# Moving the closing VectorE pair of each scan tile behind the next tile's product, in a Mamba and MoE layer

## The reference

```python
DS, DI = 16, 2048
xc = silu(conv(xs) + conv_b)             # from xz = xn @ W_in.T, split in xs and z
dt = softplus(dt_lo @ W_dt.T + b_dt);  A = -exp(A_log)
def step(h, inp):
    dt_t, B_t, C_t, x_t = inp
    dA = jnp.exp(dt_t[:, :, None] * A)
    h = dA * h + (dt_t * x_t)[:, :, None] * B_t[:, None, :]
    y = jnp.einsum('bdn,bn->bd', h, C_t)
    return (h, y)
y = ys + xc * D                          # ys: y of all time steps
y = y * jax.nn.silu(z)
out = jnp.einsum('bld,od->blo', y, W_out)
```

## Time and profile before

| | |
|---|---|
| median of 3 runs | 15,503.3 us (15,497.5 to 15,504.8) |
| profiled execution | 15,524.0 us |
| its span, slowest core (7) | 15,522.5 us |
| spans of the eight cores | 15,439.4 to 15,522.5 us |
| busy share: DVE, PE, ACT, POOL | 42%, 28%, 23%, 14% |

### The profile page before, as it was taken

The page is one execution under the profiler, slowest core; times in us unless marked ns, Lnnn a source line. Parts: engine busy times, 40 slices in busy tenths (PEclk is TensorE's granted clock), DMA queues, the critical chain, the costliest instruction groups (busy, mean ns, idle before and its releaser), DMA issues.

```text
span 15522.5 us, 107041 instructions; the slowest of 8 cores (15439.4 to 15522.5 us)
## 1 busy us (share of the span) xinstructions
PE 4382.8 (28%) x27328; PEld 2571.4 (17%) x27328; DVE 6503.0 (42%) x9337; ACT 3570.8 (23%) x6962; POOL 2140.8 (14%) x1028
## 2 busy tenths in 40 slices
PE   0001202202112012022021120120656656666666
PEld 0000101101001001011010010010433433433433
DVE  0005464454554554644545545546323322322332
ACT  1113333333332233322332332332110110100100
POOL 0001131121221211311212212113000000000000
PEclk9995555555555555555555555555576576576566
DMA  2221101101011011011010110110021021021022
GB/s 83 91 83 30 36 0 36 31 5 36 19 17 36 6 30 36 0 36 31 5 36 18 18 36 6 30 36 0 25 71 40 32 71 49 25 68 49 29 65 55
DMA packets 511228, 544.30 MB, mean 35 GB/s; under 512 B 77089, under 2 KB 437665, under 8 KB 494242
## 3 DMA queue, kind: packets, MB, share of 16 engines
q1 hardware_dynamic: 510626, 537.44, 14.1%
HBM read 407.21 MB, written 79.69 MB: 31 GB/s over the span
## 4 chain that ended last, share of the span: by engine, by line
DVE 35%; PE 21%; POOL 14%; DMA 9%; issue 9%; ACT 5%; SPq 5%; DVEq 1%; POOLq 0%; ACTq 0%
DVE h_i L551 16%; PE pb L979 7%; POOL red_a L565 7%; SPq L54 5%; POOL red_b L571 4%; DVE U_all L539 4%; DVE prod_s L561 4%; PE pb L857 3%; PE pb L890 3%; POOL red_c L576 2%; DVE f_h2e L972 2%; PE pb L599 2%; DMA we_b<-p_slab_bf 1%; DMA p_slab<-we 1%; POOL y_s L581 1%
## 5 line engine op out<-in xcount | busy, mean ns | idle before, releaser
L547 ACT ACTIVATE dA<-dt_fm,A_sb 128x256 f32<-128x256 f32 x4096 | 2075.5, 507 | 4809.7 <-DVE h_i L551 4541.8
L551 DVE TENSOR_TENSOR_SCAN h_i<-dA,hstate,U_all 128x256 bf16<-128x256 f32 x4096 | 2857.5, 739 | 153.9 <-ACT dA L547 16.1
L599 PE MATMUL pb<-ytot_bf,woutT_sb 128*128 128x256 bf16 x2048 | 349.1, 312 | 7041.4 <-DVE ytot_bf L588 7041.4
L565 POOL TENSOR_TENSOR red_a<-prod_s 128x2048 f32<-128x2048 bf16 x256 | 1035.2, 4044 | 8631.9 <-DVE prod_s L561 8631.9
L599 PEld LDWEIGHTS pb<-ytot_bf,woutT_sb 128*128 128x128 bf16 x2048 | 221.8, 108 | 7147.4 <-issue 7109.8
L979 PE MATMUL pb<-f_h2e,f_we 128*128 128x512 bf16 x4096 | 1039.7, 419 | 456.8 <-DVE f_h2e L972 456.8
L584 DVE SCALAR_TENSOR_TENSOR pr_s<-xc_bf,D_sb,y_s 128x256 f32<-128x256 bf16 x256 | 124.1, 485 | 2323.7 <-POOL y_s L581 2323.7
L453 PE MATMUL pb<-xnA_fm,winbuf 128*128 128x256 bf16 x4096 | 835.1, 363 | 543.5 <-ACT xs_scr L460 421.6
L972 DVE TENSOR_TENSOR f_h2e<-f_h2fm,f_gbc 128x4096 bf16<-128x4096 bf16 x128 | 293.4, 2292 | 1058.3 <-PE pb L979 938.7
L539 DVE TENSOR_TENSOR U_all<-Bbc,udt_fm 128x4096 bf16<-128x4096 bf16 x256 | 585.2, 2286 | 275.6 <-DMA Bbc<-dblBC_bf 275.6
L453 PEld LDWEIGHTS pb<-xnA_fm,winbuf 128*128 128x128 bf16 x4096 | 490.7, 123 | 885.8 <-issue 732.6
(11 more groups left out here) (146 smaller groups left out, 5553.0 us busy)
## 6 DMA issues: line engine op xcount, KB each, us to landing
winbuf<-winT_b SPq DMA_DIRECT2D x2048, 64.0 KB, 2.0
f_we<-we_b SPq DMA_DIRECT2D x128, 1024.0 KB, 5.0
p_slab<-we SPq DMA_DIRECT2D x64, 512.0 KB, 3.4
p_slab<-winT SPq DMA_DIRECT2D x32, 512.0 KB, 4.2
we_b<-p_slab_bf SPq DMA_DIRECT2D x128, 128.0 KB, 1.8
x_tm<-x SPq DMA_DIRECT2D x16, 1024.0 KB, 5.8
xn_scr<-xn_tm SPq DMA_DIRECT2D x16, 1024.0 KB, 4.4
Bbc<-dblBC_bf SPq DMA_DIRECT2D x256, 64.0 KB, 5.6
```

Of the source, the lines that this page charges most:

```text
L547: ex = P.add("scalar", lambda e, i=i, n=n, sl=idx % 2: e.activation(dA_s[sl][:], dt_fm[:, i, :], AF.Exp, bias=0.0, scale=A_sb[:, i * DS + ...
L551: tts = P.add("vector", lambda e, i=i, n=n, idx=idx: e.tensor_tensor_scan(h_i[:, n, :], dA_s[idx % 2][:], U_all[:, n, :], hstate[:, i * DS ...
L565: reda = P.add("gpsimd", lambda e: e.tensor_tensor(red_a[:, 0:8, :].rearrange("p a b -> p (a b)"), prod_s[:, 0:8, :].rearrange("p a b -> p ...
L599: mm = P.add("tensor", lambda e, mo=mo, i=i, b=bank: e.matmul(b[:, 0:TCM], woutT_sb[:, i * DM + mo * 128:i * DM + (mo + 1) * 128], ytot_bf ...
```

## The change

The closing pair of a tile (L584, L588) is no longer issued right behind the tile's own sums. It is kept in `pend` and issued by `flush_fin` one tile later, behind prod_s of the next tile and ahead of that tile's y_s in the program. The pair of tile 15 is flushed behind the loop. The dependencies of each instruction are the same as before.

```diff
--- before.py
+++ after.py
@@ -535,6 +535,17 @@
                     prev_f1 = None
                     hsave_prev = None
                     prev_reda = None
+                    pend = None
+
+                    def flush_fin(iq, yf):
+                        nonlocal prev_f1
+                        f1 = P.add("vector", lambda e, i=iq: e.scalar_tensor_tensor(
+                            pr_s[:], xc_bf[:, i, :], D_sb[:, i:i + 1], y_s[:],
+                            ALU.mult, ALU.add), after=[yf, fin[iq - 1] if iq > 0 else None])
+                        prev_f1 = f1
+                        fin[iq] = P.add("vector", lambda e, i=iq: e.tensor_tensor(
+                            ytot_bf[:, i, :], pr_s[:], zsil[:, i, :], ALU.mult),
+                            after=[f1, zs_done[iq]])
                     for i in range(ID):
                         uall = P.add("vector", lambda e, i=i: e.tensor_tensor(
                             U_all[:, 0:DS, :], Bbc[:, 0:DS, :],
@@ -578,16 +589,15 @@
                             red_b[:, 0:2, :].rearrange("p a b -> p (a b)"),
                             red_b[:, 2:4, :].rearrange("p a b -> p (a b)"), ALU.add),
                             after=[redb])
+                        if pend is not None:
+                            flush_fin(*pend)
+                            pend = None
                         yfin = P.add("gpsimd", lambda e: e.tensor_tensor(
                             y_s[:], red_c[:, 0, :], red_c[:, 1, :], ALU.add),
                             after=[redc, prev_f1])
-                        f1 = P.add("vector", lambda e, i=i: e.scalar_tensor_tensor(
-                            pr_s[:], xc_bf[:, i, :], D_sb[:, i:i + 1], y_s[:],
-                            ALU.mult, ALU.add), after=[yfin, fin[i - 1] if i > 0 else None])
-                        prev_f1 = f1
-                        fin[i] = P.add("vector", lambda e, i=i: e.tensor_tensor(
-                            ytot_bf[:, i, :], pr_s[:], zsil[:, i, :], ALU.mult),
-                            after=[f1, zs_done[i]])
+                        pend = (i, yfin)
+                    flush_fin(*pend)
+                    pend = None
 
                     s1_parts = []
                     prev_ads = [None, None]
```

## The result

| | before | changed |
|---|---|---|
| median | 15,503.9 us | 14,968.9 us (14,959.7 to 14,971.6) |
| ratio, 95% interval | | 0.9652 [0.9642, 0.9663] |
| span of the profiled execution | 15,522.5 us | 14,969.7 us |

The change makes the kernel 3.5% faster, 535 us. The prediction said 15,340 us, a gain of 163 us. The direction was right and the time lies between its serial case and its half-price case B, but outside the likeliest case's own range (15,160 to 15,540 us), and the gain is more than three times the forecast.

What follows compares the result with a forecast made beforehand. VectorE and GpSimd were taken to bound the kernel by taking turns, with VectorE waiting 2323.7 us for y_s. Serial turns would save only pauses, 0.68 x 240 = 163 us, giving 15,340 us; range 13,290 to 15,560 us.

Steps and rivals of the forecast that it cites:

- serial case: GpSimd sums and VectorE instructions hold each other up entirely; only pauses around sums saved, 163 us; likeliest, chance 0.40.
- half-price case B: Rival: engines share operand reads finely, VectorE at about half speed during sums; 1166 us gained, about 14,340 us; chance 0.13.
- Step 1: VectorE's wait for y_s: gone in 15 of 16 tiles, 2178.5 us, if GpSimd keeps its speed.
- Step 2: Last tile of a chunk: its wait stays whole, but tile 14's closing pair now lies inside it, 15 us.
- Step 3: New waits, at prod_s for red_a and at y_s for the moved L584: cost nothing.
- Step 4: GpSimd sums beside VectorE: from free to wholly serial; serial taken in its middle, gain only 163 us.
- Rival A: Free overlap: the sums run beside the scans at no cost, 2193 us gained, 13,310 us; chance 0.27.
- Rival C: Turns change inside the scan loop, each costing over 0.085 us; at 0.15 us, 125 us slower, 15,628 us; chance 0.11.
- D: Rival: GpSimd always loses its turn, wait reappears at L561 or L584; 15,500 us, no measurable change; chance 0.09.

Runs made afterwards that it cites:

- e3: Changed kernel with closing pair and next tile's U_all issued ahead of prod_s, so all four sums run beside scans, dA in SBUF: 14,974.4 us.
- e5: Changed kernel with closing pair and next U_all ahead of prod_s, plus red_a split into four sums of 512 elements: 14,885.9 us.
- e4: Changed kernel with closing pair and next U_all ahead of prod_s, and dA in PSUM instead of SBUF: 13,224.2 us.
- e9: Changed kernel's order with the sums over states made by TensorE matmuls into PSUM, GpSimd idle, dA in SBUF: 13,167.9 us.
- e2: Changed kernel with the dA buffers in PSUM instead of SBUF: 14,534.1 us, ratio 0.9381 to the kernel before.
- e6: Changed kernel with pr_s in a PSUM bank, so ytot_bf has one SBUF input: 14,903.5 us, ratio 0.9612 to the kernel before.

## Why the prediction was wrong

Step 1 was right. VectorE no longer waits for y_s except at the 16 chunk ends, and the 256 long waits are gone.

Step 2 was right within 4 us. The last wait is there, and the pair of tile 14 in front of it, though held by red_a like every other ytot_bf, ends inside it: from the end of the last prod_s to the last ytot_bf there are 10.3 us now and 10.1 before. The 15 us show in the second tile, which now has no pair.

Step 3 was right: no long wait at prod_s, and y_s of GpSimd does not wait for pr_s.

Step 4 had the right mechanism and the wrong size, and that is where the prediction failed. It took the serial end in its middle, only the pauses saved, 0.68 us a tile, 163 us. The traces show turns by whole instruction, as that end assumes, but the tile lost 2.08 us. The missing term is how long a sum really keeps VectorE out. I charged its whole record, 8.36 us for four. Measured are 7.02: 3.65 for red_a's 4.04, 2.14 for red_b's 2.34, and 1.23 for the 1.98 of red_c and y_s. With that, 17.38 + 7.02 is the tile of the trace within 0.06 us. The saving at the sums, which I gave as the extreme (0.18 us a sum, 0.72 a tile), is real and twice that: up to 0.39 us a sum, about half in its overlap with the instruction ahead and half at its end (e3), 8.36 - 7.02 = 1.34 us a tile in the changed kernel. (The 0.68 us are five pauses in the earlier trace rows, not four; the sum is right.) Against it I had set up to 1.2 us for changes of turn, from a pause between two sums as the nearest row; that price does not exist (e5). Two opposite corrections, one real and one not, were let cancel.

14 tiles x 2.08 us x 16 chunks are 466 us. The second tile of each chunk has no pair to hold and takes 23.24 us from the end of one prod_s to the end of the next against 26.42, 3.2 us less, 51 us in all: 0.91 of it is the missing pair. Together 517 of the 535 us. Over all tile steps of the two traces, from one prod_s to the next within a chunk, the sum falls from 6,371.7 to 5,837.9 us, 534 us, so nearly the whole gain lies there.

Rival A (free overlap) is what one gets when only instructions with at most one SBUF input run beside the sums, or no sum runs on GpSimd: its 13,310 us stand against 13,224 in e4 and 13,168 in e9. Rival B gave 14,340 us by fine sharing; no instruction shares finely. Rival C, slower, and D, no change, are excluded by the interval. The row evidence that I used for a common limit (the second input makes a VectorE instruction slower) pointed the right way but could not size anything.

## What to carry to other kernels

When a change lets GpSimd and VectorE work together, count on each engine the instructions that read SBUF on GpSimd and that have two SBUF inputs on VectorE: they take turns by whole instructions, and the gain here was only the pauses and up to 0.39 us of each GpSimd instruction. Before moving a wait, look at the operands of what will run beside the sums. With the scans' dA in PSUM the same reordering gained 6% instead of 3.5% (e2), and 15% once all sums stood beside scans (e4); with the helper work on TensorE it gained 15% as it stood (e9). A sum that costs VectorE 4.6 us of its own is not relieved by lending it to GpSimd, where it keeps VectorE out for 7.0 us.

## What the runs showed that I had not expected

A GpSimd sum that takes its turn behind a scan keeps VectorE out for 0.38 or 0.39 us less than its record alone, whatever its size (e3, for 1024, 512 and 256 elements); red_a, issued 0.04 us after the scan's record began, kept it out for only 0.15 us less. Splitting a sum into four (e5) lengthened GpSimd's work and shortened VectorE's hold by 0.66 us a tile. With pr_s in PSUM (e6) the hold only moved from ytot_bf to U_all, but a tile lasts 23.74 us there (red_a at 1526.34 and at 1550.08), 0.6 us less. A GpSimd memset of 2048 elements (1.80 us) left the two VectorE instructions beside it at their own lengths. ScalarE's exponential is 30 ns shorter when it writes to PSUM (477 against 507 ns), and sixteen scans follow each other in 11.36 instead of 11.58 us, which made the kernel before 0.34% faster with no other edit.
